# Second attention layer: the value matmuls of a key tile as one piece of 512 columns on odd beats, and the copy of the sums ahead of the exponentials

## The reference

```python
q, k, v = jnp.split(x @ W_qkv + b_qkv, 3, axis=-1)      # 16 heads of 8 features
bias   = slopes[:, None, None] * minimum(idx[None, :] - idx[:, None], 0)
scores = einsum('bhtd,bhsd->bhts', q, k) * scale + bias[None]
w = softmax(scores, axis=-1)                             # over 512 keys, no mask
y = einsum('bhts,bhsd->bhtd', w, v)
x = x + ga * (y @ W_proj + b_proj)
```

## Time and profile before

| what | value |
|---|---|
| runs of the kernel before | median 1028.89 us of 3 (1027.29 to 1029.31) |
| the profiled execution | 1028.94 us, of which the span is 1027.2 us |
| granted TensorE clock, mean over the span | 0.981 of full speed |
| busy share of the span: TensorE matmuls, VectorE, ScalarE, GpSimd | 91%, 76%, 73%, 53% |
| attention of layer 1, first maximum matmul to last copy of sums | 588.53 to 954.46 us |

### The profile page before, as it was taken

How to read it: one execution, slowest core, us unless ns; L and a number is a source line. 1 busy time by engine, 2 the same in 40 slices (tenths; PEclk the granted TensorE clock), 3 DMA queues, 4 the chain that set the end, 5 groups by cost and what they waited for, 6 DMA issues and landing times. The chain is left out here.

```text
span 1027.2 us, 23002 instructions
## 1 busy us (share of the span) xinstructions
PE 931.0 (91%) x8664; PEld 513.0 (50%) x8664; DVE 776.5 (76%) x1319; ACT 747.8 (73%) x1380; POOL 541.3 (53%) x755
## 2 busy tenths in 40 slices
PE   4789989889888999999999799999999999989896
PEld 3234343343436888888888533333333333333575
DVE  4778878878864776767777678979788898994476
ACT  2388878878786566666665488888888888889663
POOL 4376766677632121322111078687777869666343
PEclk8599999999999999999999999999999999999999
DMA  7323332221104522425233021211202021100011
GB/s 181 96 74 121 114 104 78 74 76 50 51 26 124 167 82 74 114 90 148 61 106 96 20 84 30 59 35 53 75 14 77 13 84 35 56 13 14 25 32 52
DMA packets 63598, 73.91 MB, mean 72 GB/s; under 512 B 14136, under 2 KB 46008, under 8 KB 63104
## 3 DMA queue, kind: packets, MB, share of 16 engines
q1 hardware_dynamic: 62336, 69.23, 23.5%
q10 hardware_dynamic: 1152, 3.21, 1.0%
HBM read 39.24 MB, written 2.77 MB: 41 GB/s over the span
## 5 line engine op out<-in xcount | busy, mean ns | idle before, releaser
L872 ACT ACTIVATE at_E<-at_Sb 128x512 f32<-128x512 f32 x832 | 440.9, 597 | 75.7 <-PE at_Sb L718 70.2
L944 DVE TENSOR_REDUCE mx<-at_Mb 128x2 f32<-128x1024 f32 x242 | 280.6, 1216 | 40.3 <-PE at_Mb L681 39.1
L718 PE MATMUL at_Sb<-QP,KP 64*128 64x512 bf16 (+3 forms) x1024 | 202.3, 342 | 16.7 <-ACT full_k L419 7.1
L766 PE MATMUL at_Ob<-at_E,VP 128*32 128x256 f32 (+2 forms) x2816 | 204.5, 371 | 2.2 <-POOL at_E L1046 1.0
L1046 POOL TENSOR_TENSOR at_E<-at_E,factor 128x512 f32<-128x512 f32 x128 | 162.3, 1273 | 65.3 <-ACT at_E L872 55.7
L681 PE MATMUL at_Mb<-KP,QP 62*128 62x512 bf16 x996 | 169.7, 348 | 8.5 <-DVE mx L944 6.5
L947 DVE TENSOR_REDUCE mx<-at_Mb 128x2 f32<-128x768 f32 (+1 forms) x128 | 136.7, 1085 | 52.9 <-PE at_Mb L681 51.8
L1057 POOL TENSOR_SCALAR_AFFINE_SELECT at_E<-at_E 128x512 f32<-128x512 f32 x128 | 80.0, 645 | 71.8 <-ACT at_E L872 71.8
L718 PEld LDWEIGHTS at_Sb<-QP,KP 64*128 64x128 bf16 x1024 | 73.5, 95 | 82.6 <-ACT at_E L872 37.9
L766 PEld LDWEIGHTS at_Ob<-at_E,VP 128*32 128x32 f32 x2816 | 58.2, 108 | 88.1 <-issue 65.6
L1498 DVE TENSOR_TENSOR ex_hh<-ex_R,ex_th 128x512 f32<-128x512 f32 x88 | 64.6, 734 | 49.4 <-ACT ex_th L1435 48.7
(11 more groups left out here) (213 smaller groups left out, 1441.8 us busy)
## 6 DMA issues: line engine op xcount, KB each, us to landing
QP<-q SPq DMA_DIRECT2D x96, 128.0 KB, 2.4
KP<-k SPq DMA_DIRECT2D x91, 128.0 KB, 2.4
ex_R<-rw_dram SPq DMA_DIRECT2D x32, 256.0 KB, 3.5
ctxN<-Oev SPq DMA_DIRECT2D x16, 256.0 KB, 2.5
denB<-rdram SPq DMA_DIRECT2D x64, 64.0 KB
ex_R<-rw_dram SPq DMA_DIRECT2D x16, 224.0 KB, 3.5
ex_R<-rw_dram SPq DMA_DIRECT2D x16, 192.0 KB, 3.3
ex_R<-rw_dram SPq DMA_DIRECT2D x16, 160.0 KB, 2.8
```

The source lines that it names most:

```text
L718: return pe.matmul(out[:, at:at + SEQ - q0], KP[p0:p0 + ROWS_H, b % 2, 2 * g + a, kt * P:(kt + 1) * P], QP[p0:p0 + ROWS_H, b % 2, 2 * g + ...
L766: last = pe.matmul(Ob[VW * i:VW * (i + 1), 0, q0:q1], weights_of(b, G, kt, i, q0), moving, start=(kt == 0 and q0 == 0), stop=False, skip_g ...
L872: nc.scalar.activation(dst, src, ACT.Exp).then_inc(s["s_read"], 1)
L944: v.tensor_reduce(mx[:, G % 2, :, t % 2, t // 2], src, AX.X, ALU.max).then_inc(s["m_read"], 1)
```

## The change

The eight pieces of layer 1 become four, one for each key tile, all of 512 columns, at offsets 5, 7, 9 and 11, which are t = 5, 7, 1 and 3. `NCH` becomes 4 and `CH_DONE` follows. `OEV_AT` stays 12, since 1 is added, and so does `END`. On ScalarE `read_O` of layer 1 moves ahead of the exponentials of its beat. The projection of q of batch 1 moves from beat 3 to beat 2. Layer 0 keeps its tables and its order.

A piece of 512 columns that crosses its diagonal block is cut as before: 128 + 384 columns for tile 0, 256 + 256 for tile 1, 384 + 128 for tile 2 and 512 for tile 3.

```diff
-                  {6: ((0, 0, 256), (0, 256, 512)), 7: ((1, 0, 256),), 8: ((1, 256, 512),), 9: ((2, 0, 256),),
-                   10: ((2, 256, 512),), 11: ((3, 0, 256),), 12: ((3, 256, 512),)})
+                  {5: ((0, 0, 512),), 7: ((1, 0, 512),), 9: ((2, 0, 512),), 11: ((3, 0, 512),)})
         NCH = sum(len(c) for c in CHUNKS.values())
-        OEV_AT = max(CHUNKS)
+        OEV_AT = max(CHUNKS) + (0 if causal else 1)
         END = BEATS + OEV_AT - BPG + 1
...
-        EARLY = {0: "ln", 2: "q", 5: "k"} if causal else {0: "ln", 3: "q", 6: "k"}
+        EARLY = {0: "ln", 2: "q", 5: "k"} if causal else {0: "ln", 2: "q", 6: "k"}
...
-        CH_DONE = (2, 4, 5) if causal else (2, 4, 6, 8)
+        CH_DONE = (2, 4, 5) if causal else (1, 2, 3, 4)
...
             for beat in range(START, END):
+                done, off = divmod(beat - OEV_AT, BPG)
+                if not causal and off == 0 and 0 <= done < ALLG:
+                    read_O(done)
                 for _, G, t, c in slots_S(beat):
                     exp(G, t, c)
...
-                G, off = divmod(beat - OEV_AT, BPG)
-                if off == 0 and 0 <= G < ALLG:
-                    read_O(G)
+                done, off = divmod(beat - OEV_AT, BPG)
+                if causal and off == 0 and 0 <= done < ALLG:
+                    read_O(done)
```

## The result

The changed kernel takes 1040.24 us (median of 4, 1039.29 to 1040.70) against 1028.09 us (median of 4 in the same comparison), a ratio of 1.0118 with a 95% interval of 1.0100 to 1.0135. It is slower by 12 us; forecast were 1039.2 us, 10.3 us more than before, and a range of 1031 to 1047. The profiled execution took 1040.05 us with a span of 1038.3 us.

A forecast was written before the change was run, and what follows sets the result against it. TensorE and ScalarE starving each other over three `Sb` banks bound the kernel. Batches 1 to 5 add 7.4 us, batch 6 0.8, batch 7 1.1 and 1.0, batch 0 nothing: 1028.9 + 10.3 = 1039.2 us, range 1031 to 1047.

The forecast's parts named there:

- the ring of three banks: TensorE and ScalarE, `Sb` banks: scores, exponential, bank release, second score, values form a closed loop of 2.61 us a pair.
- Plain pair: Even beat without values plus odd beat with 512 columns, M to M: 2.61 us, before 2.22.
- Pair at t = 4: Beats t = 4, 5: the maxima's transpose takes a slot, so scores wait for a second exponential: 3.10 us.
- Pairs of the fourth group: Fourth group of a batch, with norm's transpose, q and k: pairs of 3.10, 3.18, 4.44, 2.64, together 13.36 us.
- Batches 1 to 5: Layer 1: each batch 47.29 us against 45.81, 1.48 more, so 7.4 us in all.
- Batch 6: No norm, q and k, but the spike phase's transpose: 45.21 us against 44.42, 0.8 more.
- Batch 7 to beat 240: First two groups of batch 7: 21.86 us against 20.78, 1.1 more.
- Tail: From the end of batch 7's first two groups to the last copy: 23.2 us against 22.17, 1.0 more.
- read_O at no cost: Moved copy on ScalarE ends 0.62 after M, before exponentials could start at 0.65: cost zero, otherwise 0.48 a group.
- 0.65 us of idle ScalarE a pair: ScalarE needs 1.96 us of a 2.61 us pair, so it idles 0.65.
- GpSimd at beat 1, at nothing: Diagonal product behind k's split ends just when needed: costed at nothing, at most 0.5 us a batch.
- The rival by the Trainium skill, TensorEngine Tiling (Array Packing), Tiling Modes, Key Properties: TensorE: fewer changes of kind win, 23 us less (1006), or 1016 if VectorE holds the pace; chance 0.08.

The follow-up runs named there:

- the kernel with even pieces: Kernel before the change, with its eight values pieces of 256 columns spread one on each of offsets 5 to 12: 1026.02 us, ratio 0.9969.

## Why the prediction was right

The mechanism was the forecast one: the ring of three banks closes at 2.61 us a pair. The time was 1.0 us from the forecast, the difference less near: 10.3 us forecast, 11.5 in the traces and 12.2 between the medians. That the time came out nearer is luck: in this comparison the kernel before was 0.8 us faster than the median that the forecast starts from. By its own steps, prediction first:

- **Plain pair** 2.61, measured 2.61; each link to 0.01. The plain group 10.93, measured 10.95.
- **Pair at t = 4** 3.10, measured 3.10. **Value projection** 3.18, measured 3.17. **Pairs of the fourth group** 3.10, 3.18, 4.44, 2.64, measured 3.10, 3.13, 4.43, 2.66. **Output projection** 3.18, measured 3.26, the largest error of a pair.
- **Batches 1 to 5** 7.4 us, measured 7.3. A little luck is in it: the changed batch has 47.35 and not 47.29, but the kernel before has 45.89 on average and not the 45.81 of the one batch that I had read. **Batch 6** 0.8, measured 1.3 (its third group has 12.22 and not 11.85, with pairs of 2.93 and 3.42 at beats 18 and 20, where the spike phase's statistics stand on VectorE, which I had left out; its second group 11.61 and not 11.50). **Batch 7 to beat 240** 1.1, measured 1.5; why was not looked for. **Tail** 1.0, measured 1.05. **Batch 0** nothing, measured 0.34.
- **read_O at no cost**: right, but for beat 28, where it stood in my sum of 4.44 without my naming it as its price; the run with the copy put back shows 0.48 there.
- **0.65 us of idle ScalarE a pair**: 0.55 in the row above. The 0.10 is the tail of an exponential, 0.60 long in a slot of 0.49.
- **GpSimd at beat 1, at nothing**: the pair there has 2.63, 0.02 more. As soon as an experiment shortened the ring, this place bound.

The rival by the Trainium skill, TensorEngine Tiling (Array Packing), Tiling Modes, Key Properties (a change of tiling mode drains the TensorE) fits the rows (0.24 us for each change of kind; that it is a drain, no run here shows), and it did not decide: 3 x 0.24 us a group were saved on TensorE and came back as its waits for ScalarE; the kernel with even pieces pays one more change a group and is faster. The Trainium skill, Perfetto Trace Analysis, Optimization Strategy (consistent bubbles can mean too little PSUM), had the better of it: once a plain pair ScalarE idles 0.55 us, and TensorE, which is the engine that the page means (the one that should be saturated), 0.25.

That the ring sets the time, and not ScalarE's work, is shown from both sides: an exponential shortened inside the ring gives 12.9 us in the layer, one outside 0.9. A fourth bank for `Sb`, which by this account would open the ring, was not tried: it would have to come from the four of `Mb` or the one of `Ob`. So that three banks are too few is argued, not shown.

## What to carry to other kernels

When two engines hand tiles to each other through n buffers, write down the ring: fill, latency, read, release of the slot n back, and all that stands on the filling engine between there and the next fill. Work spread evenly between the fills hides in it; the same work in one block adds itself to it, even if it is cheaper as a block, and moving the block within the order only moves the ring. Before you shorten a link, see what the next bound is: here VectorE stood 0.35 us behind a ring of 2.61 (2.26 a pair), and GpSimd at beat 1 of a batch only just behind it.

## What was not expected

Halving the values gave 17 and not 43 us, and with less work on TensorE its granted clock fell twice within 25 us. Each time TensorE had just stood idle: 1.67 us up to 818.87, waiting for GpSimd, and 1.27 us up to 835.34, waiting for VectorE, in windows of 4 us in which its matmuls were busy 2.08 and 2.29 us. The clock was then 0.91 and 0.66 of full speed in the windows at 816 and 820 us, and 0.57 at 836. Between the two levels 2.4 and 1.2 GHz, 0.66 is about two thirds of the window at the lower one.

The batch took 3.6 to 3.8 us more than its neighbours, and the clock is the smaller part of it. Against batch 4, the two pairs that end with the waits are longer by 1.24 and 1.52 us, the two that follow at the lower clock by 1.09 and 0.72; other pairs gave 0.8 back. From 600 us to 965 the kernel before and the changed one have 1.00. Putting a block into a wait, with the ring unchanged, cost 29 us, most of it at the places where other work had used that wait.
